# A dead write behind each of GpSimd's first 146 indirect DMAs in a graph attention and mixture-of-experts kernel

## Chip, cores and metric

One NeuronCore of a Trainium2 chip. The metric is the device time of the launch in microseconds, lower is better: 972.01 us before (median of 3 runs, 971.95 to 973.24).

## What is computed

Two layers over 3125 nodes of 256 features, 50000 edges sorted by their target. Everything is float32.

```python
# layer 1: graph attention, 8 heads, mean over heads
h = (layernorm(x) @ W).reshape(N, 8, 256)
a_src = einsum('nhc,hc->nh', h, att_src); a_dst = einsum('nhc,hc->nh', h, att_dst)
e = leaky_relu(a_src[src] + a_dst[dst], 0.2)
alpha = softmax of e over the edges of one dst
x = x + segment_sum(h[src] * alpha, dst).mean(heads) + bias
# layer 2: 8 experts, each node to its best 2
t = layernorm(x)
x = x + t + sum over the 2 experts of weight * (gelu(t @ w1[e] + b1[e]) @ w2[e] + b2[e])
```

## The kernel before

The program is written by hand, engine by engine, with semaphores between them; each engine runs its own list in order. SP and ScalarE (ACT) issue the plain DMAs. GpSimd (POOL) issues the indirect ones, whose rows are chosen by an index in SBUF. POOL's list is what sets the order around the change.

**Start.** x, W and the attention vectors are loaded, the nodes are normalised (`xn`), turned and multiplied by the heads' vectors to give a source score and a target score for each node and head. `node_table` in HBM gets a row for each node: 256 features and 8 source scores (1056 bytes). Meanwhile the kernel finds where the edges of each target begin: ACT counts, for 25 tiles of 128 nodes, the blocks of 128 edges before each node (`blocks_counted`), and POOL *looks up* with 25 indirect DMAs the block of targets in which each node begins (`node_block`, L766 in five batches, `LOOK_UPS`). VectorE (DVE) counts inside these blocks (L1565, L1566) and so gets `starts_at`, the place of each target's first edge (`starts_ready`).

**Scores of targets.** With `starts_at` and the target scores (`score_ready` 2, DVE L1480 for the second time), POOL *scatters* them with 25 indirect DMAs to `starts_table` (L827, semaphore `starts_sent`). SP waits for all 25, loads the table back (L606, `starts_in`), DVE fills each target's score along its edges (L1689, 8 scans), TensorE (PE) turns them (L1026), ACT copies them to `score_d` (L1279). POOL also gathers one more small tile, `start_rows` (L831).

**Gathers.** The 392 blocks of edges are handled in 9 groups (`GROUP_PLAN`: seven of 48 blocks, then 32 and 24). POOL *gathers* for each block 128 rows of `node_table` into `ring` (L774, semaphore `got`), which holds two whole groups. A gather of group g from 2 on waits, at every fourth block, until PE is done with the same places of group g-2 (`block_done`). Groups 0 and 1 find the ring empty, so nothing holds their gathers back. 32 gathers of group 0 stand before the scatters; its other 16 and all 48 of group 1 behind them.

**A group.** DVE needs the group's gathers (`scores`, L1728) and then does the softmax over the group's edges (`flags`, `local_softmax`, `join_pieces`, `divide`, `weigh`), with small products by PE between. Then it builds weights for four blocks at a time (`spreads`, L1835) and PE adds the blocks into PSUM (`add_block`, L1035), from which ACT drains sums to `agg_table` (L1303 to L1310).

**After the groups.** PE projects the sums (L1161), the nodes are normalised and routed, and 56 jobs of 128 rows each run through an expert and are added to `out` by POOL's indirect DMAs (L887). The change touches nothing there.

In DVE's list nearly each instruction goes through `link`, which raises a semaphore of DVE's own and waits for it. POOL has the same helper with `pool_chain`. `job_i` is a small integer tile of 128x56 in SBUF; its last reader is POOL's own copy at L752.

Of the kernel before, what the change touches and what calls it, by code (L numbers as in the profile page):

```python
# [68 lines left out]
def gat_moe_kernel(nc, x, src, dst, W, att_src, att_dst, gnn_bias, router_w, w1, b1, w2, b2, out):  # L69
# [68 lines left out]
    with ExitStack() as ctx:  # L138
        def sb(name, shape, dt=F32):
            return ctx.enter_context(nc.sbuf_tensor(name, shape, dt))  # L140

        def sem(name):
            return ctx.enter_context(nc.semaphore(name))
# [74 lines left out]
        keep, reset, first_mask, last_mask, buf_F, buf_M, buf_X, buf_U, buf_N, buf_R, _ = (  # L218
            arena[:, o + n * SCAN:o + (n + 1) * SCAN] for n in range(NSCAN))
# [168 lines left out]
        job_i = sb("job_i", [P, JOBS], I32)  # L388
# [42 lines left out]
        dve_chain, pool_chain = sem("dve_chain"), sem("pool_chain")  # L431
# [87 lines left out]
        def slot_of(b):  # L519
            return (b + SLOT0) % ROOM  # L520
# [10 lines left out]
        def got_of(g):  # L531

            return g % 2 if g < GROUPS - 2 else g - GROUPS + 4
# [173 lines left out]
        def _(pool):  # L707
            count = [0]

            def link(ins):  # L710
                count[0] += 1
                ins.then_inc(pool_chain, 1)
                pool.wait_ge(pool_chain, count[0])

            pool.memset(xn[:, FULL, :], 0.0).then_inc(last_rows_zeroed, 1)
            link(pool.memset(ident[:, :], 0.0))
            pool.affine_select(out=ident[:, :], in_=ident[:, :], compare_op=ALU.not_equal, fill=1.0, base=0,
# [40 lines left out]
            for t0, t1 in LOOK_UPS:  # L758
                pool.wait_ge(blocks_counted, t1)
                link(pool.tensor_scalar(block_at[:, t0:t1], counted[:, t0:t1], 2.0 - NB, 0.5, ALU.max, ALU.mult))  # L760
                link(pool.tensor_scalar(block_of[:, t0:t1], block_at[:, t0:t1], 0.5 * NB - 1.0, None, ALU.add))
                link(pool.tensor_copy(block_of_i[:, t0:t1], block_of[:, t0:t1]))
                if t0 == 0:
                    pool.wait_ge(dst_stored, 16)
                for t in range(t0, t1):
                    pool.indirect_dma_start(node_block[:, t, :], None, block_rows,  # L766
                                            bass.IndirectOffsetOnAxis(block_of_i[:, t:t + 1], 0)).then_inc(node_block_in, 16)

            def gather(g, first, last):
                for s in range(first, last):  # L770
                    if g >= 2 and s % QUAD == 0:
                        pool.wait_ge(block_done, first_of[g] - ROOM + s + QUAD + 1)
                    b = first_of[g] + s
                    pool.indirect_dma_start(rows[:, slot_of(b), :], None, node_table,  # L774
                                            bass.IndirectOffsetOnAxis(idx[:, b:b + 1], 0)).then_inc(got[got_of(g)], 16)

            def far_blocks(g):
                pool.wait_ge(alpha_ready, g + 1)
# [41 lines left out]
            pool.wait_ge(xn_stored, 16 * (TILES // UNROLL))  # L820
            pool.wait_ge(va_summed, 2)
            gather(0, 0, FIRST_GATHERS)
            pool.wait_ge(score_ready, 2)
            pool.wait_ge(starts_ready, 1)
            pool.wait_ge(starts_zeroed, 16)
            for t in range(TILES):
                pool.indirect_dma_start(starts_table, bass.IndirectOffsetOnAxis(starts_at[:, t:t + 1], 0),  # L827
                                        score_all[:, t, H:2 * H], None).then_inc(starts_sent, 16)
            pool.wait_ge(w_router_done, 1)
            pool.wait_ge(target_scores_stored, 16)  # L830
            pool.indirect_dma_start(start_rows[:, :], None, score_table,  # L831
                                    bass.IndirectOffsetOnAxis(start_idx[:, 0:1], 0)).then_inc(start_rows_in, 16)
            gather(0, FIRST_GATHERS, GB)
            pool.wait_ge(steps_ready, 1)
            gather(1, 0, GB)
            for g in range(2, GROUPS - 1):
                far_blocks(g - 2)
# [574 lines left out]
        def _(dve):  # L1412
# [492 lines left out]
            def normalise(t0, tiles):  # L1905
                a = slice(t0, t0 + tiles)
                link(dve.tensor_tensor(mean[:, a], stats[:, a, 1], stats[:, a, 4], ALU.add))
                link(dve.tensor_scalar(mean[:, a], mean[:, a], 0.5, None, ALU.mult))
                link(dve.tensor_tensor(half[:, a], stats[:, a, 1], stats[:, a, 4], ALU.subtract))
                link(dve.tensor_scalar(half[:, a], half[:, a], 0.5, None, ALU.mult))  # L1910
                link(dve.tensor_tensor(half[:, a], half[:, a], half[:, a], ALU.mult))
                link(dve.tensor_tensor(rstd[:, a], stats[:, a, 2], stats[:, a, 5], ALU.add))
                link(dve.scalar_tensor_tensor(rstd[:, a], rstd[:, a], 1.0 / D, half[:, a], ALU.mult, ALU.add))
                inv_sqrt(link, rstd[:, a], rstd[:, a], half[:, a], inv_tmp[:, a])
                link(dve.scalar_tensor_tensor(half[:, a], mean[:, a], -1.0, rstd[:, a], ALU.mult, ALU.mult))
                dve.tensor_scalar(inv_tmp[:, a], rstd[:, a], 1.0, None, ALU.add).then_inc(norms_ready, 1)
                dve.wait_ge(norms_ready, [stop for _, stop in NORMS].index(t0 + tiles) + 1)
# [300 lines left out]
```

## Time and profile before

| what | value |
|---|---|
| median of 3 runs | 972.01 us |
| profiled execution, from its first to its last instruction | 1111.2 us |
| PE busy | 718.4 us (65%) |
| DVE busy | 659.9 us (59%) |
| POOL busy | 615.4 us (55%), 680 instructions |
| ACT busy | 389.4 us (35%) |
| gathers L774 | 392, 958 ns each, 375.7 us |
| scatters L827 | 25, 24.3 us |
| look-ups L766 | 25, 24.8 us |
| chain that ended last | PE 33%, DVE 27%, issue 14%, another core or an unknown queue 13% |

The profile is of one execution of its own, and it is 139.2 us longer than the median of the timed runs; the page has no other time for it than its span. Busy time is that of the engine's datapath. "Idle before" is the time the engine stood still before an instruction, with what ended it, as far as semaphore records tell; "issue" is a wait that the profile cannot lay to anything, and "remote" (in the chain: "another core or an unknown queue") one that ended by something that it did not record on this core. The kernel runs on one core.

### The profile page before, as it was taken

To read this page: it belongs to the slowest core of one execution; us is meant where nothing else is said; L and a number is where in the kernel's file an instruction comes from. 1 tells how busy PE (TensorE), PEld (TensorE's weight loads), DVE (VectorE), ACT (ScalarE), POOL (GpSimd) and SP (SyncE) were. 2 spreads that over 40 slices of the span, in tenths; PEclk is the share of its full clock that TensorE was granted. 3 is DMA by queue.
4 is the path that set the end of the run, shared out by engine and by line. 5 is a ranking of instruction groups with operands and counts; after the bars stand their busy time and mean duration, and the time that the engine had idled before them with its cause. 6 is when DMAs were issued, how large, how long until landed. Compare 5 with 4: busy or idle time off the path is not lost.

```text
span 1111.2 us, 16087 instructions
## 1 busy us (share of the span) xinstructions
PE 718.4 (65%) x3704; PEld 640.2 (58%) x3705; DVE 659.9 (59%) x1859; ACT 389.4 (35%) x884; POOL 615.4 (55%) x680
## 2 busy tenths in 40 slices
PE   5783330026474566455565366769999998669995
PEld 4782320025364456455565365768888887558985
DVE  6682470554456456454556665875687878654663
ACT  6521011016463444332312111101354423547763
POOL 6666767706656666566666665001614422476686
PEclk9999555558776777787786677888999999789998
DMA  9633054417676666565554544333999785357763
GB/s 338 201 87 77 4 144 110 113 45 229 203 232 192 199 216 196 155 191 166 168 161 135 154 130 131 117 147 128 395 331 342 279 313 174 110 136 118 120 100 41
DMA packets 97019, 189.64 MB, mean 171 GB/s; under 512 B 22975, under 2 KB 55090, under 8 KB 96092
## 3 DMA queue, kind: packets, MB, share of 16 engines
q0 software_dynamic: 31680, 70.52, 26.3%
q1 hardware_dynamic: 50704, 76.07, 20.2%
q10 hardware_dynamic: 14544, 42.02, 9.7%
q8 instruction: 35, 0.57, 0.2%
q14 instruction: 56, 0.46, 0.1%
HBM read 124.75 MB, written 64.74 MB: 171 GB/s over the span
## 4 chain that ended last, share of the span: by engine, by line
PE 33%; DVE 27%; issue 14%; another core or an unknown queue 13%; DMA 6%; ACT 3%; ACTq 1%; DVEq 1%; POOLq 1%; POOL 0%; SPq 0%; PEld 0%; PEldq 0%
PE banks L1161 13%; PE banks L1035 12%; DMA out<-ring 4%; PE banks L1201 3%; PE banks L1214 2%; DVE banks L1440 2%; DVE arena L1835 1%; PE banks L952 1%; PE banks L966 1%; DMA ring<-in_x 1%; ACT arena L1303 1%; ACT banks L1307 1%; DVE arena L1765 1%; ACTq L1289 1%
## 5 line engine op out<-in xcount | busy, mean ns | idle before, releaser
L774 POOL DMA_INDIRECT ring<-node_table,idx x392 | 375.7, 958 | 217.8 <-issue 110.8
L1035 PE MATMUL banks<-arena,ring 128*128 128x160 f32 x1568 | 298.7, 356 | 114.6 <-ACT banks L1309 51.6
L1035 PEld LDWEIGHTS banks<-arena,ring 128*128 128x128 f32 x1568 | 277.5, 234 | 135.5 <-issue 134.7
L1303 ACT COPY arena<-banks 128x400 f32<-128x400 f32 x200 | 88.5, 494 | 389.5 <-PE banks L1035 133.2
L1161 PE MATMUL banks<-ring 128*128 128x264 f32 x544 | 123.1, 386 | 0.0
L1161 PEld LDWEIGHTS banks<-ring 128*128 128x128 f32 x544 | 103.0, 190 | 17.4
L1835 DVE TENSOR_TENSOR arena<-hot,banks 128x640 f32<-128x640 f32 x84 | 65.0, 817 | 79.2 <-PE banks L1035 39.4
L887 POOL DMA_INDIRECT out<-ring x56 | 89.4, 1596 | 32.3 <-DVE ring L2129 12.3
L1201 PE MATMUL banks<-ring 128*128 128x128 f32 x448 | 65.0, 291 | 16.1 <-issue 14.7
L1201 PEld LDWEIGHTS banks<-ring 128*128 128x128 f32 x448 | 60.9, 203 | 24.6 <-issue 17.6
L1214 PE MATMUL banks<-arena,ring 128*128 x224 | 61.8, 400 | 6.4 <-ACT ring L1357 5.8
L873 POOL DMA_INDIRECT slot_table<-arena,slots x50 | 52.1, 1042 | 15.1 <-issue 13.7
L1042 PE MATMUL banks<-ident,edge_e 128*128 128x128 f32 x25 | 7.4, 426 | 79.4 <-issue 75.1
L1161 PE MATMUL banks<-ring,arena 128*128 128x264 f32 x256 | 58.4, 387 | 0.0
L1307 ACT COPY banks<-zeros 128x400 f32<-128x400 f32 x100 | 50.6, 506 | 11.0 <-ACT arena L1303 5.5
L2129 DVE SCALAR_TENSOR_TENSOR ring<-banks,job_w,ring 128x256 f32<-128x256 f32 x56 | 27.1, 484 | 45.1 <-PE banks L1214 32.6
L1161 PEld LDWEIGHTS banks<-ring,arena 128*128 128x128 f32 x256 | 48.5, 190 | 8.2
L1042 PEld LDWEIGHTS banks<-ident,edge_e 128*128 128x128 f32 x25 | 4.1, 207 | 81.9 <-issue 77.3
L869 POOL COPY arena<-tags 128x3 f32<-128x3 f32 x25 | 4.7, 187 | 81.8 <-DVEq L1985 80.6
L1309 ACT COPY banks<-zeros 128x400 f32<-128x400 f32 x100 | 49.9, 499 | 0.0
L1323 ACT COPY ring<-ring 128x448 f32<-128x448 f32 x30 | 28.9, 1014 | 51.7 <-DMA ring<-agg_table 36.6
L1214 PEld LDWEIGHTS banks<-arena,ring 128*128 128x128 f32 x224 | 40.2, 200 | 11.7 <-issue 7.7
(437 smaller groups left out, 1153.5 us busy)
## 6 DMA issues: line engine op xcount, KB each, us to landing
agg_table<-arena ACTq DMA_DIRECT2D x100, 400.0 KB
ring<-agg_table SPq DMA_DIRECT2D x25, 1600.0 KB
ring<-slot_table SPq DMA_DIRECT2D x56, 130.0 KB
ring<-node_table,idx POOLq DMA_INDIRECT x392
ring<-in_x SPq DMA_DIRECT2D x8, 640.0 KB, 10.9
ring<-in_L_gnn_W SPq DMA_DIRECT2D x4, 1024.0 KB, 7.4
arena<-in_L_ffn_w SPq DMA_DIRECT2D x16, 256.0 KB
node_table<-ring SPq DMA_DIRECT2D x5, 640.0 KB
```

What stands on the lines that cost most here:

```text
L774: pool.indirect_dma_start(rows[:, slot_of(b), :], None, node_table, bass.IndirectOffsetOnAxis(idx[:, b:b + 1], 0)).then_inc(got[got_of(g)] ...
L873: pool.indirect_dma_start(slot_table, bass.IndirectOffsetOnAxis(slots[:, k, t:t + 1], 0), tn[t % TN_RING], None).then_inc(sent[t % TN_RING ...
L887: pool.indirect_dma_start(out, bass.IndirectOffsetOnAxis(xs[j % XS_RING][:, D:D + 1].bitcast(I32), 0), ybuf[j % Y_RING], None, bounds_chec ...
L1035: m = pe.matmul(columns[:, k, bass.ds(at * (UNIT * H), SPREAD * H)], lhs[:, k * P:(k + 1) * P], weights, start=False, stop=True, skip_grou ...
L1161: m = pe.matmul(bank[proj_bank(t)][:, 0:CN], aggt[t % AGG_RING][:, k * H + h, :], W_sb[:, k, h, :], start=(k == 0 and h == 0), stop=(k == ...
L1201: m = pe.matmul(h_bank[j % 2][:, f * P:(f + 1) * P], w1_now[j % 2][:, k, f * P:(f + 1) * P], xsT[j % 2][:, k, :], start=(k == 0), stop=(k ...
L1214: m = pe.matmul(y_bank[j % 2][:, 0:D], h_sb[j % 2][:, f, :], w2_sb[:, bass.ds(e, 1), f, :].rearrange("p e n -> p (e n)"), start=(f == 0), ...
L1303: act.copy(stage[j][:, k * SLOTS * H:(k + 1) * SLOTS * H], views[k]).then_inc(drained, 1)
L1307: act.copy(views[0], zeros[:, 0:1].to_broadcast([P, SLOTS * H]))
L1309: act.copy(views[1], zeros[:, 0:1].to_broadcast([P, SLOTS * H])).then_inc(acc_free, 1)
L1323: a = act.copy(to[:, k, :, :, OVER:HOME], raw[t % RAW_RING][:, :, k, OVER:HOME, :].rearrange("p v n h -> p h v n"))
L1835: dve.tensor_tensor(spread[:, s:s + QUAD, :].rearrange("p s (d h) -> p s d h", h=H), hot[:, q * QUAD:(q + 1) * QUAD, :].unsqueeze(3).to_br ...
```

## The change

Three places in POOL's list get a call of a new helper, `pause`. It waits until POOL's last linked instruction has raised `pool_chain`, and then writes zeros to `job_i`, which nobody reads any more, with a raise of `pool_chain` in its turn. It does not wait for its own write: that is left to the next pause. One stands behind each of the 25 look-ups, each of the 96 gathers of groups 0 and 1, and each of the 25 scatters: 146 in all. `start_rows` and the gathers of groups 2 to 8 get none.

```diff
+            def pause(times=1):
+
+                for _ in range(times):
+                    pool.wait_ge(pool_chain, count[0])
+                    count[0] += 1
+                    pool.memset(job_i[:, :], 0).then_inc(pool_chain, 1)
+
...
                 for t in range(t0, t1):
                     pool.indirect_dma_start(node_block[:, t, :], None, block_rows,
                                             bass.IndirectOffsetOnAxis(block_of_i[:, t:t + 1], 0)).then_inc(node_block_in, 16)
+                    pause()
...
                     pool.indirect_dma_start(rows[:, slot_of(b), :], None, node_table,
                                             bass.IndirectOffsetOnAxis(idx[:, b:b + 1], 0)).then_inc(got[got_of(g)], 16)
+                    if g < 2:
+                        pause()
...
             for t in range(TILES):
                 pool.indirect_dma_start(starts_table, bass.IndirectOffsetOnAxis(starts_at[:, t:t + 1], 0),
                                         score_all[:, t, H:2 * H], None).then_inc(starts_sent, 16)
+                pause()
```

POOL's list before, from the last batch of look-ups to the test that stands ahead of group 2 (a row with xN stands for N equal instructions):

```order
L762 CAST block_of_i<-look_room 128x8
L766 DMA arena<-dst_table,block_of_i 128x128 x8
L774 DMA ring<-node_table,idx 128x264 x32
L827 DMA starts_table<-score_all,starts_at 53376x8 x25
L831 DMA start_rows<-score_table,start_idx 98x8
L774 DMA ring<-node_table,idx 128x264 x64
L779 TENSOR_LOAD far
```

The same list in the changed kernel, around the border between the 32 gathers and the scatters (line numbers are up to 11 higher there; L720 is the write of `pause`, L782 the gather, L837 the scatter):

```order
L782 DMA ring<-node_table,idx 128x264
L720 MEMSET job_i 128x56
L782 DMA ring<-node_table,idx 128x264
L720 MEMSET job_i 128x56
L837 DMA starts_table<-score_all,starts_at 53376x8
L720 MEMSET job_i 128x56
```

Nothing changes places: runs of DMAs back to back have become DMA and write by turns. The lists of the other engines are the same but for line numbers.

## Rows read from the trace of the kernel before

**Rows 1.** The span; then the chain that ended last, by engine.

```profile
core 0: 1111.2 us, clock 0.812
PE 33%; DVE 27%; issue 14%; another core or an unknown queue 13%; DMA 6%; ACT 3%; ACTq 1%; DVEq 1%; POOLq 1%; POOL 0%; SPq 0%; PEld 0%; PEldq 0%
```

**Rows 2.** Timeline of POOL: start us, us, instruction, idle before it and its releaser.

```profile
51.56 0.94 POOL L766 DMA_INDIRECT arena<-dst_table,block_of_i  x1 [0.30 <-issue]
59.42 0.94 POOL L774 DMA_INDIRECT ring<-node_table,idx  x1 [6.91 <-DVEq L1466]
...
99.32 0.95 POOL L774 DMA_INDIRECT ring<-node_table,idx  x1 [0.30 <-issue]
105.47 1.02 POOL L827 DMA_INDIRECT starts_table<-score_all,starts_at  x1 [5.21 <-DVE score_all L1480]
...
136.10 0.96 POOL L827 DMA_INDIRECT starts_table<-score_all,starts_at  x1 [0.30 <-issue]
143.09 1.19 POOL L831 DMA_INDIRECT start_rows<-score_table,start_idx  x1 [6.02 <-PE banks L1015]
144.58 1.02 POOL L774 DMA_INDIRECT ring<-node_table,idx  x1 [0.31 <-issue]
...
223.84 0.94 POOL L774 DMA_INDIRECT ring<-node_table,idx  x1 [0.30 <-issue]
249.94 0.94 POOL L774 DMA_INDIRECT ring<-node_table,idx  x1 [25.16 <-PE banks L1035]
...
689.02 0.94 POOL L774 DMA_INDIRECT ring<-node_table,idx  x1 [0.30 <-issue]
```

**Rows 3.** Timeline of DVE: the two long waits, group 0's scores.

```profile
72.27 3.49 DVE L1565 TENSOR_TENSOR arena<-arena,banks 128x3200 f32<-128x3200 int32 x1
...
104.83 0.37 DVE L1480 TENSOR_TENSOR score_all<-banks,rstd 128x200 f32<-128x200 f32 x1 [15.54 <-remote]
...
192.19 0.58 DVE L1706 TENSOR_TENSOR arena<-dst_scan 128x385 f32<-128x385 int32 x1 [29.89 <-remote]
...
196.78 0.56 DVE L1728 TENSOR_TENSOR edge_z<-ring,arena 128x384 f32<-128x384 f32 x1
```

**Rows 4.** Timeline of DVE, group 5: scores, three unknown waits, weights, and the next group's start.

```profile
551.83 0.55 DVE L1706 TENSOR_TENSOR arena<-dst_scan 128x385 f32<-128x385 int32 x1
...
556.40 0.43 DVE L1728 TENSOR_TENSOR edge_z<-ring,arena 128x256 f32<-128x256 f32 x1
...
562.59 0.95 DVE L1746 TENSOR_TENSOR_SCAN arena<-arena,banks 128x384 f32<-128x384 f32 x1 [3.93 <-remote]
...
585.16 0.25 DVE L1772 COPY piece_all<-banks 8x96 f32<-8x96 f32 x1 [9.51 <-remote]
...
597.69 0.19 DVE L1797 TENSOR_TENSOR piece_out<-banks,chunk_sel 128x32 f32<-128x32 f32 x1 [2.33 <-remote]
...
601.95 0.82 DVE L1835 TENSOR_TENSOR arena<-hot,banks 128x640 f32<-128x640 f32 x1 [0.23 <-issue]
...
621.72 0.56 DVE L1706 TENSOR_TENSOR arena<-dst_scan 128x385 f32<-128x385 int32 x1
```

**Rows 5.** Timeline of POOL: a look-up, small instructions between two look-ups; a write.

```profile
4.90 0.20 POOL L731 MEMSET ones_sq<- 128x128 f32 x1 [0.15 <-POOL dst_scan L729]
...
17.99 0.96 POOL L766 DMA_INDIRECT arena<-dst_table,block_of_i  x1 [0.31 <-issue]
18.96 0.31 POOL L760 TENSOR_SCALAR look_room<-look_room 128x3 f32<-128x3 f32 x1
...
19.90 0.19 POOL L762 CAST block_of_i<-look_room 128x3 int32<-128x3 f32 x1
20.37 1.04 POOL L766 DMA_INDIRECT arena<-dst_table,block_of_i  x1 [0.28 <-POOL block_of_i L762]
```

**Rows 6.** POOL by lines: writes on job_i's shape and on a longer tile.

```profile
L745 POOL IOTA job_i<- 128x56 int32 x1 | 0.2, 174 | 0.1
L729 POOL MEMSET dst_scan<- 128x386 int32 x2 | 0.8, 420 | 0.1
```

## The prediction

> **What bounds the kernel now.** I began with the span and the chain that ended last. The profiled execution spans 1111.2 us, the timed runs have a median of 972.0. That is 139.2 us apart, and 13% of the chain, some 145 us, is "another core or an unknown queue" [rows 1], though the kernel has one core. So I first looked where that time lies and what POOL does then, since the change is on POOL alone.
>
> POOL's timeline is the view to start from [rows 2]. A reader should see a strict beat: an indirect DMA takes 0.95 us, then 0.30 us pass, then the next one starts, 1.25 us from start to start (1.27 for a scatter). 32 gathers run from 59.42 to 100.27, 25 scatters from 105.47 to 137.06, `start_rows` and 64 gathers from 143.09 to 224.78. Then POOL waits 25.16 us for PE, because the ring is full.
>
> DVE's timeline over the same time shows the unknown waits [rows 3]: 15.54 us before the second L1480, which only needs PE's products, and 29.89 us before L1706, while PE, ACT and DVE stand still and only POOL works. The first ends 4.6 us behind the end of a run of gathers. Inside a later group they return: 3.93 + 9.51 + 2.33 = 15.8 us of the 69.9 us from one L1706 to the next [rows 4]. All lie where POOL issues without a rest.
>
> So there are two readings of the same rows. Either the unknown waits belong to the execution that was recorded, or they are there in every run. By size I take the first: about 145 us of the chain are unknown, and the runs are 139 us shorter. Taking the waits out, a group costs DVE and PE 69.9 - 15.8 = 54.1 us [rows 4], while POOL needs 48 x 1.25 = 60.0 us for its gathers [rows 2]. Without the unknown waits **POOL's beat is the slower of the two, and bounds the groups**. A check on the whole: POOL without any wait would end its gathers at 59.4 + 32 x 1.25 + 25 x 1.27 + 1.5 + 360 x 1.25 = 582.7, where the profile has 690.0 [rows 2]. That is 107 us of the 139; the other 32 would be unknown waits behind the gathers, or cost more time there than I see. It fits, and is no proof.
>
> By the Trainium skill (Runtime: NRT & Kernel Launch, The ~15µs preamble/postamble breakdown) a profile's total stands a fixed 6.2 us or so over the time that the runtime reports. Here the two differ by 139.2 us, so the trace does not agree with that as the whole difference; by that rule the waits would be in every run, which is the last rival below.
>
> **The change, part by part.** *One pause.* It puts a small write between two DMAs. The nearest place is the border between look-up batches [rows 5]: the look-up at 17.99 ends at 18.95, and the small instruction starts 0.01 us later. The look-up behind the last small one starts 0.28 us after it and takes 1.04 us, against 0.95 in the middle of a run [rows 2]. The write itself: an IOTA that writes the same tile took 0.17 us [rows 6], a MEMSET of 128x128 took 0.20 [rows 5]; I take 0.17, the same shape. New beat: 0.95 + 0.01 + 0.17 + 0.28 + 0.09 = 1.50 us. Old beat 1.25. A pause costs **0.25 us of POOL**. Lower bound: the write hides the gap and the longer start, and only 0.16 us remain. Upper bound: the write is as long as the 386-column one, 0.42 us [rows 6], which gives 0.50. The wait in a pause is for a write that was issued a whole beat earlier, so it is met; a late semaphore would count towards the upper end.
>
> *Look-ups: 25 pauses, 6.2 us.* The last look-up ends at 52.50, POOL then waits 6.91 us until 59.42 [rows 2]. It would end at 58.7, so the first gather does not move. DVE first reads the result at 72.27 [rows 3], about 13 us later. Cost nothing; if that cover is gone (the wait for DVE L1461 is met earlier in a run without unknown waits), at most 6.2 us.
>
> *First 32 gathers: 8.0 us.* They end at 108.3 in place of 100.3. In the profile POOL then waits 5.21 us for DVE's L1480, but that had itself an unknown wait of 15.54 us before it [rows 3]; without it the target scores are there at about 90 and the scatters follow the gathers at once. All 8.0 us count.
>
> *25 scatters: 6.25 us.* SP can load `starts_table` back only behind the last one. Counts in full on POOL's chain.
>
> *The other 16 gathers of group 0 and 48 of group 1: 16.0 us.* In the profile the 25.16 us of idle time at 249.94 [rows 2] would swallow them. But that idle time is PE being late, behind the 29.89 us wait and others. Without these, group 0's last gather is issued at 132.7 + 20.0 and DVE can start its scores at about 155; from scores to first weights group 5 took 601.95 - 556.40 - 15.8 = 29.8 us [rows 4]. So PE frees the first places of the ring from about 188 on, before POOL asks at about 213. Then POOL never rests from 59 to the last gather, and these count too.
>
> *What stays.* Groups 2 to 8 issue at the old beat, and behind the last gather nothing changes. No DMA is added or enlarged, and the write goes to a dead tile. POOL does not catch up, since it is the bound: group loop 54.1 against 60.0.
>
> *Sum.* 32 + 25 + 16 + 48 = 121 pauses on the chain x 0.25 = **30.3 us**. Set against the profiled execution's own 1111.2 us it would be 1141.5 if all were exposed, but there the idle time of 25.16, 5.21 and 6.02 us hides most. For the timed runs, which by my reading have not these waits, it is 972.0 + 30.3 = **1002.3 us**. With 0.16 to 0.34 us for a pause it is 991 to 1013.
>
> A second rule of the skill speaks of dearer pauses. SBUF — State Buffer, Who interferes with whom, says that a GpSimd instruction and certain VectorE instructions lock each other out of a shared port for a whole instruction. It would lengthen some writes; the gathers' mean of 958 ns against a common 0.94 to 0.95 shows little of it here.
>
> **Rivals.**
> 1. *Only the way to group 0 counts.* If the real beat is shorter than 1.25 (about 54.1/48 = 1.13 is where it turns), DVE and PE bound the groups and POOL's delay in group 1 is caught up. Left are the pauses ahead of group 0's scores: 32 + 25 + 16 = 73 x 0.25 = 18.3 us, 990.3. For it: the recorder may stretch the 0.30 us gap. Against it: the gap is the same in crowded and empty stretches.
> 2. *No difference.* The idle time before 249.94 is there in the runs too, and the start has cover elsewhere: 972. Against it: group 0's chain goes through the scatters.
> 3. *Faster: the pauses let a backlog clear.* The waits are in every run, and come from POOL issuing without a rest, which nothing between two DMAs lets in. For it: they end soon after POOL rests, and never show behind the last gather at 690. Against it: the 139 us, and that POOL already has a 0.30 us gap. Worked out on the profile's rows: the scatters end at 146 in place of 137, `start_rows` follows at once, 16 gathers at 1.5 us end at 171.5, so group 0's scores start at about 173.5 in place of 196.8. Group 1's gathers end at 171.5 + 72 = 243.5, and its scores can start at 245.5 in place of 268.1. That is 23 us gained: 949. It decides if at least 9 us or so of the two long waits, the delay that the scatters get, exist in a timed run and go.
>
> That the change does nothing can't be: the writes stand in POOL's list.
>
> **Numbers.** Forecast (POOL bound throughout) 0.42; only group 0's way 0.22; no difference 0.08; faster 0.28. A measurement of this kernel tells about 0.2%, 2 us, from no change. So faster 0.28, same 0.08, slower 0.64. The likeliest case alone spans 991 to 1013. For 8 in 10 the range has to take in the second case and most of the third rival: 950 to 1012, which leaves out half of the faster case's own spread and the dearest pauses.
>
> **What would show it.** In the changed profile: the beat of the first groups' DMAs at 1.50 us, writes of 0.17 us; look-ups ending near 58.7 with the first gather still near 59.4; group 2's gathers at 1.25. If rival 3 holds, the waits of 15.54 and 29.89 us are gone *and* the runs are faster. If only the waits are gone and the runs slower, the waits belonged to the recording. If the pauses cost nothing, DVE's waits before L1728 stay at none and the idle time before group 2's first gather falls from 25 us by the amount of the pauses. Wrong I would be above all if the timed runs differ from the profile in something other than these waits.

## The result, and the profile after

| | before | changed |
|---|---|---|
| median of 7 runs each, us | 972.01 (971.26 to 973.24) | 974.81 (973.28 to 979.02) |
| ratio, with its 95% interval | | 1.0034 [1.0019, 1.0049] |
| profiled execution, its own time, us | | 977.29 |
| span, us | 1111.2 | 975.6 |
| mean granted TensorE clock | 0.812 | 0.845 |

The change makes the kernel slower by 0.34%: 972.01 x 0.0034 = 3.3 us by the ratio, 2.8 us by the medians. The forecast was 30.3 us. The sign is right and the size is wrong, nine to eleven times too large.

The first thing to see in the profile is that it can't be laid beside the one shown of before as it stands. The changed kernel is slower, but its span is 135.6 us shorter. Span, mean clock, busy times and the chain, as the page of the changed kernel has them:

```profile
span 975.6 us, 16233 instructions
core 0: 975.6 us, clock 0.845
PE 677.6 (69%) x3704; PEld 608.4 (62%) x3705; DVE 660.3 (68%) x1859; ACT 390.0 (40%) x884; POOL 642.5 (66%) x826
PE 30%; POOL 27%; DVE 15%; issue 12%; DMA 11%; ACT 2%; POOLq 2%; DVEq 1%; ACTq 1%; SPq 0%; PEld 0%; PEldq 0%
```

The class "another core or an unknown queue", 13% of the chain in [rows 1], is absent, and POOL has gone from 0% to 27% of it. The same kernel as before was profiled again later (run e14_before_again on chip 5, below). Its chain is the right partner, since it too has no unknown waits:

```profile
span 973.5 us, 16087 instructions
PE 31%; POOL 21%; DVE 20%; issue 13%; DMA 10%; POOLq 1%; ACT 1%; DVEq 1%; ACTq 1%; SPq 0%; PEld 0%; PEldq 0%
```

Now like stands beside like: 975.6 against 973.5, 2.1 us, with 146 instructions more. POOL is 27% of the chain in place of 21%.

POOL's timeline of the changed kernel, at the end of the look-ups and among group 0's later gathers (start, duration, instruction, idle time before it and its releaser):

```profile
52.79 0.17 POOL L720 MEMSET job_i<- 128x56 int32 x1
53.12 1.06 POOL L773 DMA_INDIRECT arena<-dst_table,block_of_i  x1 [0.16 <-issue]
54.19 0.16 POOL L720 MEMSET job_i<- 128x56 int32 x1
55.19 0.95 POOL L782 DMA_INDIRECT ring<-node_table,idx  x1 [0.84 <-DMA node_table<-score_all]
...
132.82 0.95 POOL L782 DMA_INDIRECT ring<-node_table,idx  x1 [0.16 <-issue]
133.77 0.17 POOL L720 MEMSET job_i<- 128x56 int32 x1
134.10 0.95 POOL L782 DMA_INDIRECT ring<-node_table,idx  x1 [0.16 <-issue]
...
586.92 0.95 POOL L782 DMA_INDIRECT ring<-node_table,idx  x1 [0.30 <-issue]
588.17 0.95 POOL L782 DMA_INDIRECT ring<-node_table,idx  x1 [0.30 <-issue]
```

The write is as long as forecast, 0.17 us, and starts the moment the gather ends. But the next gather starts 0.16 us behind the write's end, not 0.28, and is not longer. From start to start it is 134.10 - 132.82 = 1.28 us, where the forecast had 1.50 and the old beat was 1.25 [rows 2]. **The write lies inside the 0.30 us that POOL leaves between two DMAs anyway**, and write and rest together, 0.33 us, are only 0.03 more than that gap. The lines of the writes and of the gathers, for the whole kernel:

```profile
L782 POOL DMA_INDIRECT ring<-node_table,idx x392 | 376.6, 961 | 108.2 <-issue 100.0 <-PE banks L1046 7.0 <-DMA node_table<-score_all 0.8
L720 POOL MEMSET job_i<- 128x56 int32 x146 | 24.9, 170 | 0.1
```

DVE's long waits of [rows 3] are not there either. In the changed kernel it waits more than 10 us at a time for two things only, the load of `starts_table` and the gathers (its timeline, then the total of the second in the table of waits):

```profile
140.88 0.69 DVE L1696 COPY banks<-hot 98x512 f32<-98x512 f32 x1 [22.17 <-DMA arena<-starts_table]
338.85 0.43 DVE L1739 TENSOR_TENSOR edge_z<-ring,arena 128x256 f32<-128x256 f32 x1 [11.30 <-DMA ring<-node_table,idx]
...
DVE edge_z L1739 <- DMA ring<-node_table,idx: 56.7, 6, 12.9
```

### The profile page after: what moved, and what is told of

It is laid out like the page before. It is cut to its first block, busy times and chain, and to the rows that moved or that the text cites. A ratio compares the mean times of both kernels' runs of the same rounds, so it can differ in the third digit from the quotient of the medians.

```text
span 975.6 us, 16233 instructions
## 1 busy us (share of the span) xinstructions
PE 677.6 (69%) x3704; PEld 608.4 (62%) x3705; DVE 660.3 (68%) x1859; ACT 390.0 (40%) x884; POOL 642.5 (66%) x826
## 4 chain that ended last, share of the span: by engine, by line
PE 30%; POOL 27%; DVE 15%; issue 12%; DMA 11%; ACT 2%; POOLq 2%; DVEq 1%; ACTq 1%; SPq 0%; PEld 0%; PEldq 0%
POOL ring L782 20%; PE banks L1172 15%; PE banks L1046 9%; DMA out<-ring 7%; POOL starts_table L837 3%; POOL job_i L720 2%; PE banks L977 2%; DMA ring<-node_table,idx 2%; DVE banks L1451 1%; PE banks L963 1%; DMA ring<-in_x 1%; POOL out L898 1%; PE banks L1212 1%; ACT banks L1318 1%; PE banks L1053 1%
## 5 line engine op out<-in xcount | busy, mean ns | idle before, releaser
L782 POOL DMA_INDIRECT ring<-node_table,idx x392 | 376.6, 961 | 108.2 <-issue 100.0
L1046 PE MATMUL banks<-arena,ring 128*128 128x160 f32 x1568 | 262.8, 333 | 36.8 <-ACT banks L1320 18.9
L1046 PEld LDWEIGHTS banks<-arena,ring 128*128 128x128 f32 x1568 | 251.7, 217 | 48.5 <-issue 47.8
L1225 PE MATMUL banks<-arena,ring 128*128 x224 | 59.4, 388 | 2.2 <-DVE ring L2140 1.6
L977 PEld LDWEIGHTS banks<-va,ring 128*128 128x128 f32 x200 | 43.9, 333 | 0.4 <-DVE va L1484 0.4
## 6 DMA issues: line engine op xcount, KB each, us to landing
ring<-in_x SPq DMA_DIRECT2D x8, 640.0 KB, 11.4
```

The costliest lines, as they stand in the source:

```text
L977: m = pe.matmul(bank[a][:, t * n:(t + 1) * n], xT[:, t, k * P:(k + 1) * P], va[:, k, 0:H + NX] if a == 0 else va_of[1][:, k, :], start=(k ...
L1046: m = pe.matmul(columns[:, k, bass.ds(at * (UNIT * H), SPREAD * H)], lhs[:, k * P:(k + 1) * P], weights, start=False, stop=True, skip_grou ...
L1225: m = pe.matmul(y_bank[j % 2][:, 0:D], h_sb[j % 2][:, f, :], w2_sb[:, bass.ds(e, 1), f, :].rearrange("p e n -> p (e n)"), start=(f == 0), ...
```

## The theories

- **The beat.** POOL's beat bounds the kernel from the look-ups to the last gather, and a pause costs what it adds to the beat: 0.03 us as written, more if the DMA behind it has to wait for the write.
- **Two effects.** The pauses cost POOL time and save other time, since unknown waits exist in timed runs and shorten. The 3.3 us would be a difference of two larger numbers.
- **The recording.** The unknown waits of before come from being recorded, as the prediction took it.

The expectations below were written before their runs, and name the theories in their own words.

## The experiments

All edits are shown against the changed kernel, where the diff names no other. Kernels of one group ran on one chip, with the kernel before beside them; every ratio is against that chip's own runs of the kernel before.

### First group: e1 to e4 (chip 8)

**e1_before_again** is the kernel before, unchanged, as a test of the recording.

> The kernel before, unchanged. Theory 'recording': the unknown waits belong to an execution that is recorded in full and come back in it whenever no pauses stand in POOL's list, so the profiled span is again far above the timed runs (1080 to 1130 against 972). Rival 'chance': the first profile was an odd execution, and this one spans about 971. Both expect a ratio of 1.000. Under 'recording' the spans of the timed runs are about 970.

**e2_wait_own_write**: the DMA behind a pause waits for the write.

```diff
-                    pool.wait_ge(pool_chain, count[0])
-                    count[0] += 1
-                    pool.memset(job_i[:, :], 0).then_inc(pool_chain, 1)
+                    link(pool.memset(job_i[:, :], 0))
```

> The same 146 writes, but each pause also waits for its own write before the next DMA. Theory 'hidden write': in the changed kernel the write stands in the 0.30 us that POOL lets pass between two DMAs anyway (0.16 write, 0.16 behind it), so the beat grows by 0.025 only; once the DMA has to wait for the write's semaphore, the 0.28 us that the look-up at 20.37 showed behind a waited-for instruction return, the beat is about 1.40 to 1.50, and 121 of them cost 18 to 30 us: 990 to 1002. Rival 'covered': the pauses cost little because the start has cover, and the length of a pause does not matter: 973 to 977.

**e3_short_write**: one column is written in place of 56.

```diff
-                    pool.memset(job_i[:, :], 0).then_inc(pool_chain, 1)
+                    pool.memset(job_i[:, 0:1], 0).then_inc(pool_chain, 1)
```

> The dead write cut from 56 columns to 1 (the profile before has 0.10 us for a 128x1 MEMSET). Hidden write, with a sum: beat = DMA + write + 0.16, so 0.95 + 0.10 + 0.16 = 1.21, under the beat without pauses, and 121 x 0.04 = 5 us faster than before: 967. Hidden write, with a maximum: the gap is the larger of 0.30 and write + 0.16, so the beat is 1.25 and the time that of before, 972. Theory 'backlog' (pauses change the runs through what they let through, not through their length) keeps 975.

**e4_all_gathers**: a pause behind each of the 392 gathers.

```diff
-                    if g < 2:
-                        pause()
+                    pause()
```

> A pause also behind each of the 296 gathers of groups 2 to 8. Theory 'POOL is the bound throughout': 296 more beats of +0.025 on the path, +7.4 us over the changed kernel, 982. Rival 'only the start is on the path': 975.

| run | median, us | ratio to before on this chip |
|---|---|---|
| kernel before, 29 runs | 1131.33 (1123.35 to 1141.13) | |
| e1_before_again | 1133.01 | 1.0004 [0.9971, 1.0037] |
| e2_wait_own_write | 1107.10 | 0.9779 [0.9738, 0.9819] |
| e3_short_write | 1124.00 | 0.9935 [0.9906, 0.9963] |
| e4_all_gathers | 1120.40 | 0.9912 [0.9879, 0.9946] |

The surprise is the first line. On this chip the *timed* runs of the kernel before take 1131 us, as long as its profile, where they took 972 in the result. It is no disturbance of single runs: all 29 lie between 1123 and 1141. The profile of e1_before_again, its span, one of DVE's waits and the largest waits for the unknown:

```profile
core 0: 1134.4 us, clock 0.800
106.88 0.37 DVE L1480 TENSOR_TENSOR score_all<-banks,rstd 128x200 f32<-128x200 f32 x1 [15.79 <-remote]
...
ACT arena L1303 <- remote: 124.9, 22, 13.8
```

Its profiled execution took 1136.15 us for a span of 1134.4, in line with the other nine (1125.69 to 1137.85), so the unknown waits of [rows 3] are real time of an execution. **The theory of the recording falls**: it had expected timed runs of about 970. I call chips where this is so *chips that stall*, though each chip was used in one group of runs only, so that the chip and the hour can't be told apart.

The expectations for e2 to e4 were sums for a kernel at 972 us and can't be held against these times; the fourth group does that. Here the pauses gain. The dearest one in POOL time, e2, gains most, and neither of DVE's two early waits is left in it (L1480's counterpart starts at 83.4 us, L1706's at 158.9). In its timeline the DMA waits for the write, 0.27 us behind it, and the beat is 78.45 - 77.07 = 1.38 us:

```profile
77.07 0.95 POOL L780 DMA_INDIRECT ring<-node_table,idx  x1 [0.27 <-POOL job_i L718]
78.02 0.16 POOL L718 MEMSET job_i<- 128x56 int32 x1
78.45 0.95 POOL L780 DMA_INDIRECT ring<-node_table,idx  x1 [0.27 <-POOL job_i L718]
```

The one-column write of e3 takes 0.12 us, the DMA follows 0.19 us later, and the beat is the old one, 78.11 - 76.86 = 1.25:

```profile
76.86 0.95 POOL L782 DMA_INDIRECT ring<-node_table,idx  x1 [0.19 <-issue]
77.81 0.12 POOL L720 MEMSET job_i<- 128x1 int32 x1
78.11 0.94 POOL L782 DMA_INDIRECT ring<-node_table,idx  x1 [0.19 <-issue]
```

The number of pauses is not what counts, though. e4 has three times as many as the change, each at the short beat of 1.28 us, gains less than half of what e2 does, and both early waits still stand in it (DVE's timeline; 15.79 and 40.93 us in e1; L1490 and L1716 are L1480 and L1706 of before):

```profile
105.85 0.36 DVE L1490 TENSOR_TENSOR score_all<-banks,rstd 128x200 f32<-128x200 f32 x1 [15.69 <-remote]
192.80 0.56 DVE L1716 TENSOR_TENSOR arena<-dst_scan 128x385 f32<-128x385 int32 x1 [29.50 <-remote]
```

### Second group: e5 to e8 (chip 15)

**e5_change_again** is the changed kernel itself.

> The changed kernel, unchanged. Two regimes are known by now: one in which the kernel before takes 972 us and one in which it takes 1131. Theory 'two prices': the pauses cost 121 x 0.025 = 3 us where nothing stalls, and give back part of the stalls where engines stall while POOL issues without a rest. So if the kernel before takes some 972 here: ratio 1.003; if some 1131: ratio 0.98 to 0.99, between the short write (0.9935) and the waited-for write (0.978). Rival 'length only': +3 us in both regimes, ratio 1.003.

**e6_two_writes**: two writes to a pause.

```diff
-            def pause(times=1):
+            def pause(times=2):
```

> Two dead writes in each pause, the second waiting for the first. Hidden write: the first fits into POOL's gap, the second does not, so each pause costs another 0.17 to 0.45 us, and where nothing stalls 121 of them give 972 + 3 + 21..54: 996 to 1029. Where engines stall, the longer pause lets more through: about 1107 as the waited-for write, ratio 0.978 or less. 'Covered' expects 975 in the first regime.

**e7_gathers_only**: the pauses behind look-ups and scatters are taken out.

```diff
                                             bass.IndirectOffsetOnAxis(block_of_i[:, t:t + 1], 0)).then_inc(node_block_in, 16)
-                    pause()
...
                                         score_all[:, t, H:2 * H], None).then_inc(starts_sent, 16)
-                pause()
```

> Pauses only behind the 96 gathers of groups 0 and 1; none behind look-ups and scatters. Without stalls: 96 x 0.025 = 2.4 us, ratio 1.0025. With stalls: the waits before the second L1480 (15 us) and before L1706 (30 us) stand behind these gathers, so most of whatever the change gains must be here: two thirds or more of it.

**e8_scatters_only**: only those behind the 25 scatters stay.

```diff
                                             bass.IndirectOffsetOnAxis(block_of_i[:, t:t + 1], 0)).then_inc(node_block_in, 16)
-                    pause()
...
-                    if g < 2:
-                        pause()
```

> Pauses only behind the 25 scatters. Without stalls 25 x 0.022 = 0.6 us, ratio 1.0006. With stalls: no long wait stands in the scatters, only DVE's crawl of 1.4 us an instruction, which is not on the path there: ratio 0.998 to 1.002.

| run | median, us | ratio to before on this chip | 97th gather starts at |
|---|---|---|---|
| kernel before, 23 runs | 1118.26 | | (e1, chip 8: 255.0) |
| e5_change_again | 1108.22 | 0.9889 [0.9838, 0.9939] | 239.8 |
| e6_two_writes | 1111.42 | 0.9929 [0.9903, 0.9955] | 245.5 |
| e7_gathers_only | 1103.99 | 0.9876 [0.9836, 0.9916] | 237.3 |
| e8_scatters_only | 1115.49 | 0.9971 [0.9938, 1.0004] | 250.3 |

This chip stalls too, and the very same kernel that is 0.34% slower in the result is 1.1% *faster* here. The gain comes with the pauses behind the 96 gathers: those alone have all of it, those behind the scatters alone have none that can be told. The 97th gather, the first of group 2, waits for PE to free the ring; with the pauses behind the gathers it starts earlier than in e8 on the same chip, although POOL has more to do ahead of it. That is what the third rival described. With two writes both of DVE's early waits of [rows 3] are gone (DVE's timeline of e6_two_writes; L1491 and L1717 are L1480 and L1706 of before):

```profile
82.02 0.36 DVE L1491 TENSOR_TENSOR score_all<-banks,rstd 128x200 f32<-128x200 f32 x1
166.96 0.56 DVE L1717 TENSOR_TENSOR arena<-dst_scan 128x385 f32<-128x385 int32 x1 [1.01 <-PE banks L1037]
```

But e6 gains no more than e5, whose interval overlaps its own, and misses its expectation of 0.978 or less. Its groups 2 to 8, which have no pause, still wait for the unknown (table of its waits):

```profile
ACT arena L1314 <- remote: 102.2, 20, 12.9
DVE piece_all L1783 <- remote: 63.0, 5, 30.1
```

It also pays a longer beat in groups 0 and 1. That the two together eat up what the early waits give back is argued and not shown; e2, which cleared the same two waits on chip 8, did gain 2.2%.

### Third: e9 (chip 13)

**e9_all_wait_own**: the waited-for write of e2 behind every look-up, scatter and gather, 442 in all, meant to beat e2 on a chip that stalls.

```diff
-                    pool.wait_ge(pool_chain, count[0])
-                    count[0] += 1
-                    pool.memset(job_i[:, :], 0).then_inc(pool_chain, 1)
+                    link(pool.memset(job_i[:, :], 0))
...
-                    if g < 2:
-                        pause()
+                    pause()
```

> A waited-for write behind each of the 25 look-ups, the 25 scatters and all 392 gathers. In the traces of the earlier runs the waited-for write makes the beat 1.38 us in place of 1.25. Where nothing stalls and POOL is the bound, 417 beats x 0.13 = 54 us slower: 1026, ratio 1.056. Where engines stall while POOL issues without a rest, the later groups gain as the first two did (22 us for 146 pauses on the chip that takes 1131): ratio 0.96, or, if POOL's own beat becomes the bound there (48 x 1.38 = 66 us a group against 70), 0.98 as with pauses in the first groups alone.

It ran on a chip that does not stall: the kernel before had 973.31 there, and this one 1044.57, 1.0732 [1.0707, 1.0758], so 71.3 us slower. The last gather starts at 656.6 us, 72.1 later than in the unpaused kernel (584.5, e14 below). The mechanism of the beat fits; its size was 17 us too small. I had 0.13 us for a pause in all groups, while in groups 2 to 8 it was (656.6 - 232.1) / 295 = 1.44 against (584.5 - 210.3) / 295 = 1.27, so 0.17 us; that is 12 of the 17. Most of the other 0.04 sits in few places: nine of the 295 beats last 2.2 to 3.2 us, six of them ahead of a group's first gather, where e14 has one such beat. One of the six, POOL's timeline of e9:

```profile
437.72 0.16 POOL L718 MEMSET job_i<- 128x56 int32 x1
439.56 0.95 POOL L780 DMA_INDIRECT ring<-node_table,idx  x1 [1.68 <-issue]
```

What POOL does in these 1.68 us is open. For the theory of two effects the run says that without stalls there is no gain to set against the cost. Whether waited-for writes in all groups pay on a chip that stalls was not measured.

### Fourth group: e10 to e13, the same edits on a chip that does not stall (chip 2)

e10 is e2's kernel, e11 e4's, e12 e6's and e13 e3's; their diffs stand above.

> The 146 waited-for writes again, hoping for a chip without stalls (kernel before at 972). Beat 1.38 against 1.25, 121 on the path: 121 x 0.13 = 16 us, 988, ratio 1.016. If the length of a pause did not matter: 975. On a chip with stalls: 0.978 as before.

> The plain write behind all 392 gathers again. Without stalls and with POOL the bound throughout: 121 + 296 = 417 beats x 0.025 = 10.4 us, 982.5, ratio 1.0107. If only the start is on the path: 1.003. On a chip with stalls: 0.991 as before.

> Two writes in each of the 146 pauses again. Beat 1.46 against 1.25: 121 x 0.21 = 25 us, 997, ratio 1.026 without stalls. On a chip with stalls: 0.993 as before.

> The write of one column again. Its beat was 1.25 us (0.95 + 0.12 + 0.19), that of the kernel before, so without stalls the ratio is 1.000 (972), and the 3 us of the change are its 0.025 us a beat and nothing else. If the change's 3 us came from the waits or the semaphore traffic of the pauses: 1.003. On a chip with stalls: 0.9935 as before.

### Fifth group: e14 and e15 (chip 5)

**e14_before_again** is the kernel before, for a profile without stalls. **e15_look_ups_two_waited** has pauses behind the look-ups alone, two waited-for writes each, to see what cover these have.

> The kernel before once more, for its trace without stalls: ratio 1.000. If the pauses had nothing to do with the absence of stalls there (a matter of the chip), its profiled span is about 970 on a chip that times it at 972, has no unknown waits, POOL issues without a rest from about 54 to about 583 us, and DVE waits some 55 us for gathers. If pauses were what took the stalls out of the changed kernel's profile: span above 1100. On a chip with stalls: 1120 to 1135 again, and nothing new.

```diff
-            def pause(times=1):
+            def pause(times=2):
...
-                    pool.wait_ge(pool_chain, count[0])
-                    count[0] += 1
-                    pool.memset(job_i[:, :], 0).then_inc(pool_chain, 1)
+                    link(pool.memset(job_i[:, :], 0))
...
-                    if g < 2:
-                        pause()
...
                                         score_all[:, t, H:2 * H], None).then_inc(starts_sent, 16)
-                pause()
```

> Only the 25 look-ups get a pause, but of two writes, each waited for: some 0.13 + 0.4 = 0.5 us a look-up, 13 us in all, behind which POOL should start its gathers. 'Covered' (my step: POOL waits 6.9 us for DVE there) expects 13 - 6.9 = 6 us at most. 'Exposed' (without stalls POOL has no such wait and is the bound from the first look-up on) expects most of the 13 us: 983 to 985, less what the looks of ACT's counts cover. On a chip with stalls: within 0.5% of before.

What POOL's timelines and the runs give on the chips that do not stall (2, 5 and 13, and the one of the result, whose number is not on record). The last five columns are the starts of POOL's DMAs, less those of e14; the time is the median less that of the kernel before on the same chip:

| kernel | beat of paused gathers | time, us | ratio | 1st gather | 1st scatter | 33rd gather | 97th gather | last gather |
|---|---|---|---|---|---|---|---|---|
| e14_before_again | none paused, 1.25 | +0.1 | 1.0002 [0.9992, 1.0011] | 54.9 | 96.0 | 129.7 | 210.3 | 584.5 |
| e13_short_write | 1.25 | +0.8 | 1.0007 [0.9997, 1.0016] | -0.9 | -1.0 | -1.1 | -0.7 | -1.0 |
| the change | 1.28 | +2.8 | 1.0034 [1.0019, 1.0049] | +0.3 | +1.3 | +1.8 | +3.8 | +3.7 |
| e15_look_ups_two_waited | none paused, 1.25 | +10.7 | 1.0114 [1.0097, 1.0131] | +11.2 | +10.7 | +10.7 | +10.8 | +11.3 |
| e11_all_gathers | 1.28 | +11.6 | 1.0118 [1.0103, 1.0132] | +0.5 | +1.3 | +1.9 | +3.6 | +12.4 |
| e10_wait_own_write | 1.38 | +22.9 | 1.0228 [1.0215, 1.0242] | +3.8 | +7.4 | +10.7 | +22.5 | +21.9 |
| e12_two_writes | 1.46 | +35.7 | 1.0364 [1.0351, 1.0378] | +5.9 | +12.8 | +18.5 | +35.0 | +34.0 |
| e9_all_wait_own | 1.38 | +71.3 | 1.0732 [1.0707, 1.0758] | +2.5 | +6.7 | +9.9 | +21.7 | +72.1 |

Each row reads the same way. What the pauses add to POOL piles up from column to column, is never made good again, and is the time that the kernel loses, within 2 us (profiles are single executions on different chips; e13 shows that a start can lie 1 us off for no cause of ours). **The theory of the beat holds on these chips**, over a range of 0 to 71 us. The theory of two effects falls here: neither the changed kernel nor the kernel before has an unknown wait in its trace, and e13, with as many pauses and waits but the old beat, loses nothing that can be told. The forecast's 0.25 us for a pause is more than even e12's two writes add to the beat, 0.21.

e11, e13, e14 and e15 came out as their theory of the beat had it. Two did not, in size: e10 was expected at +16 us and lost 22.9, e12 at +25 and lost 35.7. Both sums left out the look-ups, which delay the first gather by 3.8 and 5.9 us. And the 64 later gathers of groups 0 and 1 add 22.5 - 10.7 = 11.8 us in e10 and 35.0 - 18.5 = 16.5 in e12, where 64 beats at 0.13 and 0.21 make 8.3 and 13.4; as in e9, a few beats of 1.5 to 2.8 us hold most of that difference. A piece of e12's POOL timeline:

```profile
75.62 0.95 POOL L782 DMA_INDIRECT ring<-node_table,idx  x1
76.57 0.36 POOL L720 MEMSET job_i<- 128x56 int32 x2
77.08 0.95 POOL L782 DMA_INDIRECT ring<-node_table,idx  x1
```

The profile of e14_before_again is the one that the prediction would have needed. POOL's timeline first, then DVE's, then one of its waits in sum:

```profile
52.35 1.06 POOL L766 DMA_INDIRECT arena<-dst_table,block_of_i  x1 [0.31 <-issue]
54.85 0.94 POOL L774 DMA_INDIRECT ring<-node_table,idx  x1 [1.44 <-DVEq L1466]
...
94.78 0.95 POOL L774 DMA_INDIRECT ring<-node_table,idx  x1 [0.30 <-issue]
96.03 1.02 POOL L827 DMA_INDIRECT starts_table<-score_all,starts_at  x1 [0.30 <-issue]
...
84.64 0.36 DVE L1480 TENSOR_TENSOR score_all<-banks,rstd 128x200 f32<-128x200 f32 x1
138.55 0.69 DVE L1685 COPY banks<-hot 98x512 f32<-98x512 f32 x1 [21.44 <-DMA arena<-starts_table]
149.52 0.56 DVE L1706 TENSOR_TENSOR arena<-dst_scan 128x385 f32<-128x385 int32 x1 [1.01 <-PE banks L1026]
...
DVE edge_z L1728 <- DMA ring<-node_table,idx: 55.0, 6, 12.5
```

The idle times of [rows 2] before the first gather (6.91), the first scatter (5.21) and `start_rows` (6.02) are 1.44, 0.30 and 0.30. Target scores are ready at 85 us, 11 us before POOL needs them. L1706 runs at 149.5 in place of 192.2, with 1.01 us of waiting in place of 29.89.

In e15 the last look-up starts 63.72 - 52.35 = 11.4 us later and the first gather 11.2 later; the kernel loses 10.7:

```profile
63.72 0.95 POOL L771 DMA_INDIRECT arena<-dst_table,block_of_i  x1 [0.27 <-POOL job_i L718]
64.67 0.47 POOL L718 MEMSET job_i<- 128x56 int32 x2
66.09 0.95 POOL L780 DMA_INDIRECT ring<-node_table,idx  x1 [0.95 <-POOL job_i L718]
```

## Why the prediction was right in its sign and wrong in its size

**What bounds the kernel: right.** Reading the profile without its unknown waits gave POOL as the bound from the first gather to the last. The check on the whole said that the gathers would then end at 582.7 us; in e14_before_again the last one starts at 584.5 and ends about 1 us later. That it is so close is in part luck: the check starts 4.6 us late (59.4 for 54.9), and beats that are now and then longer than 1.25 make up for it. It also had 107 us of the 139 ahead of the last gather and 32 behind it, and the spans bear this out: 689.0 - 584.5 = 104.5 ahead, and (1111.2 - 689.0) - (973.5 - 584.5) = 33.2 behind. DVE waits 55.0 us for gathers in e14, and e9 to e15 pass POOL's delays on to the kernel's end, within 2 us. The first rival (DVE and PE catch up in group 1) falls with them: 96 gathers' worth of delay is still there at the last.

**The price of one pause: wrong, and this decided the size.** The step was "0.95 + 0.01 + 0.17 + 0.28 + 0.09 = 1.50", from the border between look-up batches. Of its terms the write (0.17) and its start (at once) were right. The 0.28 was not: at that border [rows 5] the look-up *waits* for the small instruction, and the row says so, `[0.28 <-POOL block_of_i`. In `pause` nothing waits for the write. This was told ahead of the prediction, in the section on the change: the helper leaves its own write to the next pause. e10 has the wait put back, and has 0.27 us behind the write, nearly the forecast's 0.28, and a beat of 1.38. The 0.09 for a longer gather (1.04 in place of 0.95) is in neither. So a pause adds 0.17 + 0.16 - 0.30 = 0.03 us. Of the 0.22 us that the forecast had too much, 0.12 is this wait that isn't there and 0.09 the longer gather.

The lower bound, 0.16 us, failed with it. It assumed that the write hides the gap, but took the write to be on top of something. The right bound from [rows 2] was zero: a gap of 0.30 us in which POOL's datapath does nothing can hold a write of 0.17. (The upper end has a slip of its own: the bound was 0.50 us a pause, and the sum's range uses 0.34, which nothing derives.) With 0.03 the forecast's own sum is 121 x 0.03 = 3.6 us, against 3.3 measured. That is a check made with the answer known, and e11 is one made of more pauses: 295 more at 0.03 are 8.9 us, and it lost 11.6 - 2.8 = 8.8 us more.

**The look-ups "cost nothing": wrong, and without weight here.** The cover of 6.91 us was part of the stalled profile; without stalls it is 1.44 us. The prediction had named this case ("if that cover is gone ... at most 6.2 us"; the wait that it calls DVE L1461 there is L1466 in [rows 2]). e15 shows that it is the true one, with 10.7 us lost. At 0.03 us a pause all 25 are worth 0.8 us, less than the profiles tell apart.

**The other counts: right.** First gathers, scatters and the rest of groups 0 and 1 all lie on the chain: in the changed kernel the delay grows from 0.3 us at the first gather to 3.8 at the 97th, 3.5 us for 121 pauses.

**"The unknown waits belong to the execution that was recorded": wrong in its reason.** They are not there in the runs of the result, so the sum could leave them out; that part held. But a chip that stalls has them in every execution, timed or recorded. The 139.2 us between span and median are then best read as the difference between two kinds of chip, not between recorded and not. On which chip the profile of before was taken is not on record, so this is inferred, from two facts: its span of 1111.2 us lies near the 1118 us of chip 15, and in each later run the time of the profiled execution stands only 1.7 to 1.9 us above its own span, on either kind of chip: 1136.15 to 1134.4 in e1, 975.24 to 973.5 in e14, 977.29 to 975.6 for the change. The Trainium skill's rule cited ahead (Runtime: NRT & Kernel Launch, The ~15µs preamble/postamble breakdown) sets a profile's total time some 6.2 us above the runtime's time. No run here has that total, only the span from first to last instruction, so none can show the rule; the prediction set it against the span.

**The third rival** (faster, 0.28) is true on chips 8 and 15 and false on the chip of the result. It named the condition correctly: the waits have to be there in a timed run. Its size was too high, 23 us forecast against 10.0 measured (1118.26 - 1108.22): of the two waits only the second shrank (29.89 us in [rows 3], 14.00 in e5), and the first is still 21.78 us in e5, now laid to PE:

```profile
105.69 0.37 DVE L1491 TENSOR_TENSOR score_all<-banks,rstd 128x200 f32<-128x200 f32 x1 [21.78 <-PE banks L977]
```

**The second rule of the Trainium skill**, that a shared port could lengthen the writes (SBUF — State Buffer, Who interferes with whom), shows in a few rows and in no sum that matters. 14 of the 146 writes last 0.20 to 0.34 us in place of 0.16; five of them are of 0.27, between 56 and 64 us, while VectorE runs casts and tensor-scalar instructions from SBUF, and the gathers among them take up to 1.28 us. That agrees with the rule, and is no proof of it. The mean of the 146 is 170 ns.

**What stays open.** What the unknown waits are, that is, what is queued while POOL issues DMAs on a chip that stalls, and why one chip has them and another has not. No run here separates chips by anything but their number. That a longer rest between POOL's DMAs clears them fits e2 and e6, in which both early waits are gone. e4, with a pause of the short kind behind every gather, still has them both, and "they never show behind the last gather", which spoke for POOL in the prediction, is not so: in the profile of before DVE and ACT have 29 us of them there, in 8 waits, and 33 us of the difference to e14 lie there. So the gathers alone can't be all of the cause; POOL issues 106 other indirect DMAs in that last stage (L873, L887), and no run paused these. No version beat both kernels on both kinds of chip: the one-column write of e3 and e13 comes nearest, faster where chips stall (0.9935) and not to be told from before where they don't (1.0007 [0.9997, 1.0016]).

## What to carry to other kernels

Ask of an inserted instruction whether the next one *waits* for it. If it does, its duration and the semaphore's way add to the beat (0.13 us here); if not, it may fit into a gap that was there anyway, and the bound from below is zero. When a profile's span and the timed runs lie 14% apart, its idle times are no cover for anything: get a profile whose span matches the times, before a term is costed at nothing. And a change that acts on stalls can be a gain on one chip and a loss on the next, so it has to be timed on both.

## What the runs showed of the hardware

- The same program has a median of 972 to 973 us on chips 2, 5 and 13 and of 1118 and 1131 us on chips 15 and 8, and no execution of it lies between 976 and 1111. The profiles differ by unknown waits of ACT and DVE (222 and 189 us in that of before, none in e14) and by waits of PE that the profile lays to nothing (183 us against 8). Nine tenths of each lie between the first and the last gather.
- Between two indirect DMAs POOL leaves 0.30 us. A write of 0.12 us in it costs nothing (e13), one of 0.16 us adds 0.03 to the beat (the change, e11), two add 0.21 (e12). If the DMA waits for the write, it starts 0.27 us behind it (e2, e10).
- Making POOL slower by 0.13 us behind each of 146 DMAs took 2.2% off the kernel's time on a chip that stalls (e2) and added 2.3% on one that does not (e10).
